# Second attention with half-precision probabilities and values: three products each, and the values' lower halves left in the accumulator

## The reference, cut to what matters

```python
V = (values @ Wv).reshape(b, nk, H, HD).transpose(0, 2, 1, 3) * ind_v[:, None, :, None]
scores = jnp.einsum('bhqd,bhkd->bhqk', Q, K) / jnp.sqrt(jnp.float32(HD))
attn = jax.nn.softmax(scores, axis=-1)
attn = attn * ind_k[:, None, None, :]
denom = jnp.sum(attn, axis=-1, keepdims=True)
attn = attn / jnp.where(denom == 0.0, 1.0, denom)
out = jnp.einsum('bhqk,bhkd->bhqd', attn, V)
```

## Time and profile before

| | |
|---|---|
| median of 3 runs | 1221.46 us (1220.59 to 1227.62) |
| the profiled execution's own time | 1222.51 us |
| its span, first to last instruction | 1220.7 us |
| mean granted clock of TensorE | 0.887 |
| busy share of the span: PE, PEld, DVE, ACT, POOL | 75%, 57%, 59%, 46%, 50% |

### The profile page before, as it was taken

One profiled execution on the slowest core, in us unless ns is written; L12 is line 12 of the kernel. 1 busy time (PEld: TensorE's weight loads), 2 busy tenths in 40 slices (PEclk: granted clock), 3 DMA queues, 4 the chain that ended last, 5 costly groups with the idle time before them and its releaser, 6 DMA issues. The chain is left out here.

```text
span 1220.7 us, 27328 instructions
## 1 busy us (share of the span) xinstructions
PE 919.2 (75%) x10334; PEld 697.5 (57%) x10334; DVE 722.6 (59%) x1774; ACT 566.3 (46%) x928; POOL 615.9 (50%) x582
## 2 busy tenths in 40 slices
PE   3478888865676654399980378988989889995998
PEld 1357666542222221399970167877777777884565
DVE  3567766535677557255534455676667776653665
ACT  1157777756565563166650133333334343332454
POOL 1258888763777767144436834445353530111454
PEclk9998989967787877699995678999899999997999
DMA  5221222007548647777758102240422313000001
GB/s 167 75 65 55 64 76 71 8 16 277 215 187 270 274 188 263 202 212 200 203 153 320 39 25 90 93 160 24 159 90 91 112 60 141 2 2 1 19 19 35
DMA packets 112064, 144.03 MB, mean 118 GB/s; under 512 B 14325, under 2 KB 93090, under 8 KB 105794
## 3 DMA queue, kind: packets, MB, share of 16 engines
q1 hardware_dynamic: 74050, 110.81, 27.0%
q0 software_dynamic: 8192, 16.79, 4.6%
q10 hardware_dynamic: 29696, 14.68, 4.2%
HBM read 76.60 MB, written 65.40 MB: 116 GB/s over the span
## 5 line engine op out<-in xcount | busy, mean ns | idle before, releaser
L929 POOL DMA_INDIRECT fetched_a<-rows_y,chosen_row x128 | 123.0, 961 | 172.9 <-DVE att_a L822 121.2
L1486 POOL DMA_INDIRECT rows_x<-rows_r,index_r x128 | 138.2, 1079 | 67.5 <-issue 36.7
L450 POOL TENSOR_TENSOR p_lo_a<-probs_a,p_hi_a 128x1024 f16<-128x1024 f32 x64 | 136.0, 2130 | 48.6 <-ACT p_hi_a L313 48.6
L629 PEld LDWEIGHTS psum<-v_x_a,probs_a 128*128 128x128 f32 x1024 | 127.0, 200 | 3.4 <-issue 0.3
L629 PE MATMUL psum<-v_x_a,probs_a 128*128 128x65 f32 x1024 | 127.8, 280 | 0.0
L1664 POOL TENSOR_TENSOR h_lo_t<-hidden_t,h_hi_t 96x512 f16<-96x512 f32 x48 | 55.5, 1155 | 92.3 <-ACT h_hi_t L1632 92.3
L807 DVE TENSOR_REDUCE negmax_a<-psum 128x8 f32<-128x1024 f32 x64 | 78.2, 1222 | 18.8 <-PE psum L614 8.3
L312 ACT ACTIVATE probs_a<-psum 128x1024 f32<-128x1024 f32 x64 | 65.7, 1026 | 34.9 <-PE psum L170 34.9
L359 DVE TENSOR_REDUCE negmax_a<-psum 128x8 f32<-128x1024 f32 x64 | 77.8, 1216 | 5.2 <-PE psum L186 5.0
L680 PE MATMUL psum<-wo,att_t_a 128*128 128x128 f32 x512 | 63.9, 278 | 8.3 <-ACT att_t_a L741 5.8
L680 PEld LDWEIGHTS psum<-wo,att_t_a 128*128 128x128 f32 x512 | 60.6, 192 | 15.8 <-DVE comb_t L797 4.8
(11 more groups left out here) (335 smaller groups left out, 2938.1 us busy)
## 6 DMA issues: line engine op xcount, KB each, us to landing
values<-v_out_r SPq DMA_DIRECT2D x16, 1040.0 KB
v_x_a<-values SPq DMA_DIRECT2D x16, 1040.0 KB
keys<-k_out_r SPq DMA_DIRECT2D x16, 1024.0 KB
listed_t<-rows_x SPq DMA_DIRECT2D x96, 128.0 KB, 2.4
rows_y<-result_t ACTq DMA_DIRECT2D x48, 256.0 KB, 2.5
k_a_a<-keys SPq DMA_DIRECT2D x16, 512.0 KB
k_b_a<-keys SPq DMA_DIRECT2D x16, 512.0 KB
q_pad_a<-narrow_q SPq DMA_DIRECT2D x64, 64.0 KB
```

Source lines behind the costliest of these rows:

```text
L450: nc.gpsimd.tensor_tensor(p_lo[:, s % RING0, :], probs[:, s % NPR, :], p_hi[:, s % RING0, :], ALU.subtract).then_inc(s_plo, 1)
L629: last_ = nc.tensor.matmul(PV[:, part, i * (HD + 1):(i + 1) * (HD + 1)], probs[:, s % 3, lane(part, i)], v_x[:, par, b % GB, h, :], start= ...
L929: nc.gpsimd.indirect_dma_start(fetched[:, b % NF1, k, :], None, rows_y, bass.IndirectOffsetOnAxis(ap=chosen["row"][:, b, k:k + 1], axis=0) ...
L1486: nc.gpsimd.indirect_dma_start(rows_x, bass.IndirectOffsetOnAxis(ap=index[:, g * GB + t, k:k + 1], axis=0), rows[:, g % 2, t, :, :].rearra ...
```

## The change

In the second attention `probs` goes to two buffers and is split: ScalarE copies it into `p_hi` (half precision, three buffers) right after the exponential, and the remainder `p_lo` is made in two halves, columns 0 to 511 by GpSimd at the head of its step, columns 512 to 1023 by DVE after the step's maxima. `values(s)` waits for both and makes three half-precision products per head. In routing an item "v" leaves its bank twice: ScalarE writes the upper half (with the mask), TensorE subtracts that upper half from the bank with a product by minus the identity (`remainder`, 512 columns), and ScalarE copies what is left as the lower half. The order is one item behind: `remainder` of an item stands after the products (or the upper copy) of the next, and after the last of a call of `keep`. ScalarE's `keep(g, 0, 11)` becomes `keep(g, 0, 4)` and `keep(g, 4, 11)`. The bytes stored and loaded for the values are the same.

```diff
             def values(s):
-                pe.wait_ge(s_exp, s + 1)
+                pe.wait_ge(s_plo[0], s + 1)
+                pe.wait_ge(s_plo[1], s + 1)
...
-                        last_ = nc.tensor.matmul(PV[:, part, i * (HD + 1):(i + 1) * (HD + 1)], probs[:, s % 3, lane(part, i)],
-                                                 v_x[:, par, b % GB, h, :], start=True, stop=True)
+                        nc.tensor.matmul(o, p_hi[:, s % 3, lane(part, i)], v_hi, start=True, stop=False)
+                        nc.tensor.matmul(o, p_hi[:, s % 3, lane(part, i)], v_lo, start=False, stop=False)
+                        last_ = nc.tensor.matmul(o, p_lo[:, s % 3, lane(part, i)], v_hi, start=False, stop=True)
...
             def exponentials(s):
                 act.wait_ge(s_sc, s + 1)
+                if s >= 2:
+                    act.wait_ge(s_plo[0], s - 1)
+                    act.wait_ge(s_plo[1], s - 1)
+                pair = T_BANK.rearrange("p a n -> p (a n)")
+                nc.scalar.activation(probs[:, s % 2, :], pair, ACT.Exp, scale=scale).then_inc(s_exp, 1)
+                act.wait_ge(s_exp, s + 1)
                 if s >= 3:
                     act.wait_ge(s_pv, s - 2)
-                pair = T_BANK.rearrange("p a n -> p (a n)")
-                nc.scalar.activation(probs[:, s % 3, :], pair, ACT.Exp, scale=scale).then_inc(s_exp, 1)
+                nc.scalar.activation(p_hi[:, s % 3, :], probs[:, s % 2, :], ACT.Copy).then_inc(s_phi, 1)
...
+            def lower(s):
+                dve.wait_ge(s_phi, s + 1)
+                nc.vector.tensor_tensor(p_lo[:, s % 3, 512:1024], probs[:, s % 2, 512:1024], p_hi[:, s % 3, 512:1024],
+                                        ALU.subtract).then_inc(s_plo[1], 1)
...
                 if 0 <= s + LM1 < NP:
                     maxima(s + LM1)
+                if 0 <= s < NP:
+                    lower(s)
...
             for s in range(FIRST, LAST):
+                if 0 <= s < NP:
+                    pool.wait_ge(s_phi, s + 1)
+                    nc.gpsimd.tensor_tensor(p_lo[:, s % 3, 0:512], probs[:, s % 2, 0:512], p_hi[:, s % 3, 0:512],
+                                            ALU.subtract).then_inc(s_plo[0], 1)
...
+                def remainder(g, at):
...
+                    pe.wait_ge(s_v_hi, 8 * g + n + 1)
+                    upper_ = v_out[:, n // 4, 0, n // 2 % 2, n % 2 * 8:n % 2 * 8 + 8, 0:D1]
+                    nc.tensor.matmul(KV[(len(made) * g + at) % 3].rearrange("p (h d) -> p h d", d=D1), minus16[:, :], upper_,
+                                     start=False, stop=True, skip_group_check=True).then_inc(s_v_rest, 1)
...
                         last_.then_inc(s_kv, 1)
+                        if at > first:
+                            remainder(g, at - 1)
+                    remainder(g, last - 1)
...
+                def remainder(g, at):
...
+                    act.wait_ge(s_v_rest, 8 * g + n + 1)
+                    nc.scalar.activation(v_out[:, n // 4, 1, n // 2 % 2, n % 2 * 8:n % 2 * 8 + 8, 0:D1],
+                                         KV[(len(made) * g + at) % 3].rearrange("p (h d) -> p h d", d=D1),
+                                         ACT.Copy).then_inc(s_v, 1)
...
+                        if at > first:
+                            remainder(g, at - 1)
+                    remainder(g, last - 1)
...
-                    keep(g, 0, 11)
+                    keep(g, 0, 4)
+                    keep(g, 4, 11)
```

More of the change, by code:

```diff
@@ L533, in attention1 @@
     k_a, k_b = sb("k_a", [P, 2, 8, 512], F16), sb("k_b", [P, 2, 8, 512], F16)
-    v_x = sb("v_x", [P, 2, GB, H, HD + 1])
+    v_x = sb("v_x", [P, 2, 2, 2, 2, H, HD + 1], F16)
     negmax, negmax_t = sb("negmax", [P, 2, P]), sb("negmax_t", [P, 2, P], F16)
-    probs = sb("probs", [P, 3, 1024])
+    probs = sb("probs", [P, 2, 1024])
+    p_hi, p_lo = sb("p_hi", [P, 3, 1024], F16), sb("p_lo", [P, 3, 1024], F16)
     den, rden = sb("den", [P, 2, 4]), sb("rden", [P, 2, 4])
@@ L547, in attention1 @@
     s_den, s_rden, s_att = sem("den"), sem("rden"), sem("att")
+    s_phi, s_plo = sem("p_hi"), [sem(f"p_lo{n}") for n in range(2)]
     s_fetch, s_add, s_whole = [sem(f"fetch{n}") for n in range(NF1)], sem("add"), sem("whole")
@@ L628, in values @@
                         h = 2 * (4 * j + i) + part
-                        last_ = nc.tensor.matmul(PV[:, part, i * (HD + 1):(i + 1) * (HD + 1)], probs[:, s % 3, lane(part, i)],
-                                                 v_x[:, par, b % GB, h, :], start=True, stop=True)
+                        o = PV[:, part, i * (HD + 1):(i + 1) * (HD + 1)]
+                        v_hi, v_lo = (v_x[:, par, b % GB // 2, n, b % 2, h, :] for n in range(2))
+                        nc.tensor.matmul(o, p_hi[:, s % 3, lane(part, i)], v_hi, start=True, stop=False)
+                        nc.tensor.matmul(o, p_hi[:, s % 3, lane(part, i)], v_lo, start=False, stop=False)
+                        last_ = nc.tensor.matmul(o, p_lo[:, s % 3, lane(part, i)], v_hi, start=False, stop=True)
                 last_.then_inc(s_pv, 1)
@@ L1094, in experts0 @@
         c_hi, c_lo = rt("c_hi", [P, 512], F16), rt("c_lo", [P, 512], F16)
-        k_out, v_out = rt("k_out", [P, 2, 2, 4, 512], F16), rt("v_out", [P, 2, 2, H, D1 + 1])
-        s_masked, s_kv, s_kv_hi, s_kv_lo, s_v = (rsem(n) for n in ("masked", "kv", "kv_hi", "kv_lo", "v"))
+        k_out, v_out = rt("k_out", [P, 2, 2, 4, 512], F16), rt("v_out", [P, 2, 2, 2, H, D1 + 1], F16)
+        minus16 = rt("minus16", [P, P], F16)
+        s_masked, s_kv, s_kv_hi, s_kv_lo = (rsem(n) for n in ("masked", "kv", "kv_hi", "kv_lo"))
+        s_v, s_v_hi, s_v_rest = (rsem(n) for n in ("v", "v_hi", "v_rest"))
         s_k_out, s_v_out, s_parted = [rsem(f"k_out{n}") for n in range(2)], [rsem(f"v_out{n}") for n in range(2)], rsem("parted")
@@ L1147, in _ @@
             def _(pe):
+                def remainder(g, at):
+                    kind, n = made[at]
+                    if kind != "v":
+                        return
+                    pe.wait_ge(s_v_hi, 8 * g + n + 1)
+                    upper_ = v_out[:, n // 4, 0, n // 2 % 2, n % 2 * 8:n % 2 * 8 + 8, 0:D1]
+                    nc.tensor.matmul(KV[(len(made) * g + at) % 3].rearrange("p (h d) -> p h d", d=D1), minus16[:, :], upper_,
+                                     start=False, stop=True, skip_group_check=True).then_inc(s_v_rest, 1)
                 def keep(g, first, last):
@@ L1413, in _ @@
                 nc.vector.memset(top[:, :, K0:8], NONE)
+                for n in range(2):
+                    nc.vector.memset(v_out[:, n, 1, :, :, D1], 0.0)
                 nc.vector.memset(so_far[:, 0, :], 0.0).then_inc(s_set, 1)
```

13 lines of the change are left out of this document (7 added, 6 removed).

## The result

The changed kernel takes 1265.1 us (median of 4 runs, 1261.8 to 1276.4), the kernel before 1223.1 beside it: a ratio of 1.0348, 95% interval 1.0300 to 1.0396. It is slower by 42 us, where 17 had been forecast. The profiled execution took 1262.9 us, with a span of 1261.1 against 1220.7.

What follows compares the result with a forecast made beforehand. Second attention was taken as paced by TensorE with waits, routing by the index-to-index chain through DVE, ScalarE and TensorE. 1222.5 + 28 (routing) - 10 (second attention) = 1240.5, forecast 1240 us, range 1196 to 1266.

Steps and rivals of the forecast that it cites:

- The sign: Whole kernel: slower, 1240 us against a profiled 1222.5; slower was given 54%.
- the products: Second attention, TensorE: 24 half-precision products of 65 columns per step at 0.03 us each, 0.72 us instead of 1.83.
- Routing's mechanism: Routing: ranks stand behind the third "v" item's remainder, which waits for ScalarE's upper copy, so DVE's choice comes later.
- Its term: Routing: each of eight groups 3.5 us longer, +28 us in all, between +11 and +45.
- I get 0.25 us per round, plus about 0.6 ... I take 0.8 per round: Second attention: gain per eight-step round, 5 us over 7 rounds; with 5 in the tail, -10 us, between -71 and +20.
- 71: Second attention: TensorE's whole relief in us over 64 steps, 1.11 per step, taken as the ceiling.
- 1.11: Second attention: us by which cheaper products relieve TensorE per step, taken off at each `values` in a round.
- just in time: Second attention: DVE's q_a, right behind the exponential, comes 1.04 us later because of ScalarE's copy, without delaying the step.
- Costed at nothing, with up to 16 if its cover goes: Second attention: GpSimd's subtraction free as GpSimd idles 59% of the body; else up to 1.16 us twice a round.
- adding 0.65 us for `lower`: Second attention: DVE's half of the subtraction delays a step by 0.65 us where DVE's queue is the last link.
- the signs named beforehand: Second attention: products at 0.03 us pitch, `values` waiting some 0.7 us for `p_lo` in most steps, q_b later behind ScalarE's copy.
- TensorE falls cold: Rival, routing: at the lower clock "v" items cost another 2.5 to 3 us per group, 1262 us; chance 18%.

Runs made afterwards that it cites:

- experiment 1: Changed kernel with both routing `remainder` functions returning at once, so only the second attention's change remains: median 1251.9 us, 1.0255 of the kernel before.
- 4: Changed kernel with the exponential written straight to `p_hi`, `p_lo` zero, no subtraction and no ScalarE copy: 0.9965 of the kernel before.
- 11: Routing of the kernel before, second attention with the three products, no subtraction and no ScalarE copy: 0.9770 of the kernel before.
- 9: Changed kernel with the whole subtraction on GpSimd and none on DVE: 1264.4 us, 1.0283 of the kernel before.
- 10: Routing of the kernel before, changed second attention with the whole subtraction on GpSimd: 1.0040 of the kernel before.
- experiment 2: Changed kernel without GpSimd's half of the subtraction in the second attention: 1.0275 of the kernel before.
- experiment 8: Kernel before with one spare DVE subtraction of 0.68 us per second-attention step, between tiles nothing else uses: 1.0232 of the kernel before.
- 3: Changed kernel without DVE's half of the subtraction (`lower(s)`) in the second attention: median 1233.5 us, 1.0077 of the kernel before.
- 5: Changed kernel without either half of the subtraction, `p_lo` zero, ScalarE's copy to `p_hi` kept: median 1232.5 us, 1.0075 of the kernel before.
- 6: Changed kernel with DVE's half of the subtraction of odd steps moved behind the next step's first q_b: 1.0358 of the kernel before.
- 7: Changed kernel without subtraction or ScalarE copy, plus one spare DVE subtraction of 0.68 us per second-attention step: 1.0312 of the kernel before.
- 12: Kernel before with one spare ScalarE copy of the probabilities per step, right behind the exponential: 1.0105 of the kernel before.
- 18: Kernel before with routing's ranks products issued behind the second value's products instead of the third's: median of ten runs 1245.4 us, ratio 1.0048.

## Why the prediction was right and wrong

**Right.** The sign, and the products: a pitch of 0.03 us. The added instructions at 682, 1162 and 1057 ns were costed at 680, 1160 and 1040. Routing's mechanism held in the profile: the ranks stand behind the third value's remainder, and DVE waits longer for them. DVE in the third group, against 1.01 in the earlier trace rows:

```profile
346.21 0.29 DVE L1431 TENSOR_TENSOR placed_r<-psum,table_r 128x128 f32<-128x128 f32 x1 [2.87 <-PE psum L1249]
```

Its term was too large: 3.5 us per group forecast, 2.6 measured (28.0 less 25.4), 17.6 us instead of 28, inside the 11 to 45. DVE's waits for the ranks rose from 5.6 to 22.5 us, about as much. That they are the cause was not shown: every run that shortened them met the unexplained waits. What the routing costs is itself unsteady. By pairs of experiments that differ in it alone it is 0.9% (after against experiment 1), 2.0% (4 against 11), 2.4% (9 against 10): 11 to 30 us.

**Wrong: "I get 0.25 us per round, plus about 0.6 ... I take 0.8 per round", -10 us for the second attention.** It was +24 to +26. TensorE's busy time in the loop fell by 32 us and not by 71, and its waits rose from 52.3 to 108.5. In the loop's own account:

- the products, -24 us (391.0 to 367.3). The forecast took 1.11 at each `values`; 0.37 per step shows. TensorE's busy time fell by 51 us, and its waits rose by 27.
- ScalarE's copy, +11 (to 378.6). The prediction had it "just in time", at no price.
- GpSimd's half, +3.5 without DVE's half (to 382.1), +14.4 with it. Costed at nothing, with up to 16 if its cover goes.
- DVE's half, +33 beside GpSimd's (382.1 to 415.3), +22 alone (378.6 to 400.9), 28 to 40 as spare work. This is the step that failed: adding 0.65 us for `lower` and taking 1.11 for the products, as if the one paid for the other. I had seen that `lower` makes q_b 0.68 late, added it "where DVE's queue is the last link", and let the 1.11 of the next `values` pay for it. But the relief falls in steps where DVE is no longer waiting for `values`, and those waits were no slack to begin with.

Of the signs named beforehand, `values` waiting for `p_lo` by some 0.7 us came true, but in 25 steps and not in most. The profile hides it, since `values` waits for two semaphores: in the loop it names DVE's `p_lo` once, for 4.0 us, and "issue" 24 times, for 15.6 us, 0.65 each. Each of these 24 `values` starts 0.10 us after DVE's `p_lo` ended, for instance:

```profile
788.35 0.68 DVE L823 TENSOR_TENSOR p_lo_a<-probs_a,p_hi_a 128x512 f16<-128x512 f32 x1
789.13 0.19 PE L634 MATMUL psum<-v_x_a,p_hi_a 128*128 128x65 f16 x1 [0.96 <-issue]
```

Without GpSimd's half (experiment 2), where only one semaphore is left, the profile names DVE's `p_lo` for 15.0 us there, and without any half (4) under 1 us is left. The rest of the loss shows in TensorE's waits for q_b (13.8 to 23.5 us in the loop), `comb_t` (2.3 to 10.1) and others behind DVE's queue.

The rival "TensorE falls cold" was meant for routing, whose clock rose from 0.80 to 0.85. In the attention's body it fell from 0.97 to 0.90. Part of that came with the cheaper products (0.98 to 0.94 between 760 and 1060 us in experiment 4), part with the waits (experiment 8), and it makes each added wait dearer: from experiment 4 to the changed kernel TensorE's busy time rose by 19 us of the 48 with the same products. As a price of its own it stood nowhere in the sum.

## What to carry to other kernels

An engine busy 60 to 75% can set the pace in a part of the steps. Its waits in the others are no cover: price added work by the steps in which it runs without a wait, or add spare work of that size and measure (0.68 us cost 0.45 to 0.6 here). When work can lie on either of two engines, measure its price on each: the same half of a subtraction cost 33 us on DVE and 10 to 12 on GpSimd. And a conversion that relieves the busiest engine is worth only what the other engines' waits leave, here 24 of the 71 us forecast, from which every conversion is then paid. Where an instruction waits for two semaphores, compare its start with the ends of both releasers before believing that it waited for neither.

## What was not expected

- Beside GpSimd's subtraction DVE's 128 combine instructions kept their median of 352 ns, but single ones took up to 1337, where 405 is the most without it.
- Less work made routing longer: the periods of the index were 28.0 us in the changed kernel and 34.9 without ScalarE's second copy (289.1 to 533.7).
- The last index lay between 482.2 and 507.7 us in the eight kernels with the changed routing untouched (after and experiments 2 to 7 and 9), between 466.0 and 474.5 in the six with the routing of before (before and experiments 1, 8, 10, 11, 12), and runs of one kernel (18) lay 30 us apart.
